# One-core adapter, diffusion, film and attention kernel: first FFN, query, key and value products as three float32r products each

## What is computed

```python
scale, shift = split(silu(sin_emb(timestep)) @ W_ada + b_ada)
x = ln(src) * (1 + scale) + shift
q, k, v = x @ Wq + bq, x @ Wk + bk, x @ Wv + bv          # 16 heads of 16
probs = softmax(where(src_mask, -inf, q @ k.T / 4 + attention_bias))
x = x + (probs @ v) @ Wo + bo
h = ln(x) * g2 + beta2
out = x + gelu2(h @ W1 + b1) @ W2 + b2                   # 256 -> 1024 -> 256
```

## Time and profile before

| what | us |
| --- | --- |
| median of 3 runs | 933.13 (932.63 to 935.77) |
| span of the profiled execution, first to last instruction | 929.6 |
| before the first head's exponentials | 93.2 |
| turn 0 | 96.0 |
| turns 1 to 6, each | 104.4 to 104.6 |
| last turn and what follows it | 113.5 |
| PE, DVE, ACT, POOL busy | 856.0, 742.4, 727.5, 237.6 |

### The profile page before, as it was taken

How to read it: one execution, slowest core, us unless ns; L and a number is a source line. 1 busy time by engine, 2 the same in 40 slices (tenths; PEclk the granted TensorE clock), 3 DMA queues, 4 the chain that set the end, 5 groups by cost and what they waited for, 6 DMA issues and landing times.

```text
span 929.6 us, 18071 instructions
## 1 busy us (share of the span) xinstructions
PE 856.0 (92%) x5630; PEld 659.5 (71%) x5715; DVE 742.4 (80%) x2377; ACT 727.5 (78%) x1897; POOL 237.6 (26%) x236
## 2 busy tenths in 40 slices
PE   7775878999999999999999999999999999999987
PEld 6454656777777777777777777777777777777766
DVE  8556888898898898898898898898897898866542
ACT  1122978979898888979898888979898888988763
POOL 2232123224123323223123323223123323120000
PEclk9777899999999999999999999999999999999999
DMA  9813644554447363654447363554447363555400
GB/s 258 250 50 101 188 136 138 154 162 138 132 131 187 98 168 105 168 160 136 133 131 188 98 170 104 169 161 132 136 131 188 98 170 102 158 161 167 140 12 23
DMA packets 133081, 130.88 MB, mean 141 GB/s; under 512 B 18265, under 2 KB 123481, under 8 KB 132969
## 3 DMA queue, kind: packets, MB, share of 16 engines
q1 hardware_dynamic: 101616, 112.02, 42.9%
q10 hardware_dynamic: 31370, 17.71, 6.9%
HBM read 112.61 MB, written 17.07 MB: 140 GB/s over the span
## 4 chain that ended last, share of the span: by engine, by line
PE 58%; ACT 19%; DVE 7%; issue 3%; POOL 0%; ACTq 0%; DVEq 0%
PE ff_ps L1340 11%; PE ff_ps L1321 8%; PE PT_ps L1376 8%; ACT Pr L1073 5%; PE G L1144 5%; PE G L1136 5%; PE scores_ps L1361 4%; PE ctx_ps L1398 3%; ACT L1073 3%; DVE bias L931 2%; PE scores_ps L1358 2%; PE ff_ps L1307 2%; ACT tanh L1055 2%; ACT ffT L1059 2%; ACT PT L1086 2%
## 5 line engine op out<-in xcount | busy, mean ns | idle before, releaser
L1073 ACT ACTIVATE Pr<-bias,nmax 128x256 f32<-128x256 f32 x512 | 255.7, 506 | 35.0 <-DVE nmax L931 34.5
L931 DVE CUSTOM_DVE_ANT_0 bias<-scores_ps,bias 128x256 f32<-128x256 f32 x512 | 194.0, 420 | 48.1 <-PE scores_ps L1361 27.9
L1086 ACT ACTIVATE PT<-PT_ps 128x512 f32<-128x512 f32 x256 | 152.2, 595 | 51.8 <-PE PT_ps L1376 47.1
L1376 PE MATMUL PT_ps<-ident,Pr 128*128 128x128 f32 x1024 | 155.6, 274 | 8.0 <-ACT Pr L1073 8.0
L560 POOL TENSOR_TENSOR rstd<-var,half_neg 128x2 f32<-128x2 f32 (+1 forms) x64 | 43.2, 674 | 387.6 <-DVE var L684 252.4
L1376 PEld LDWEIGHTS PT_ps<-ident,Pr 128*128 128x128 f32 x1024 | 119.6, 140 | 16.8 <-ACT Pr L1073 13.2
L1321 PE MATMUL ff_ps<-ctxT,w 128*128 128x256 f32 x480 | 117.2, 387 | 12.8 <-ACT ffT L1059 10.7
L1340 PE MATMUL ff_ps<-w,ffT 128*128 128x256 f32 x480 | 113.1, 381 | 0.2 <-DVE ffT L908 0.2
L1321 PEld LDWEIGHTS ff_ps<-ctxT,w 128*128 128x128 f32 x480 | 86.3, 190 | 32.5 <-ACT ffT L1059 16.2
L1361 PE MATMUL scores_ps<-k_stack,q_stack 96*128 96x256 bf16 x512 | 98.7, 273 | 7.3 <-issue 2.1
L1073 ACT ACTIVATION_READ_ACCUMULATOR Pr<-bias,nmax 128x1 f32 x512 | 100.5, 196 | 0.0
(11 more groups left out here) (216 smaller groups left out, 1637.2 us busy)
## 6 DMA issues: line engine op xcount, KB each, us to landing
bias<-in_fside_Bx16xSxS_dram SPq DMA_DIRECT2D x256, 256.0 KB, 3.2
part_dram<-front ACTq DMA_DIRECT2D x32, 384.0 KB, 2.8
q_stack<-part_dram SPq DMA_DIRECT2D x32, 192.0 KB, 3.2
k_stack<-part_dram SPq DMA_DIRECT2D x32, 192.0 KB, 3.9
F<-in_x_dram SPq DMA_DIRECT2D x16, 256.0 KB, 3.7
ada<-rows_dram SPq DMA_DIRECT2D x16, 256.0 KB, 5.3
q_stack<-part_dram SPq DMA_DIRECT2D x32, 128.0 KB, 3.2
k_stack<-part_dram SPq DMA_DIRECT2D x32, 128.0 KB, 3.8
```

Of the source, the lines that this page charges most:

```text
L931: nc.vector.tensor_tensor_reduce(out=t, in0=SP_[:, n % 2, q * S:(q + 1) * S], in1=t, scale=-1.0, scalar=BIG, op0=ALU.add, op1=ALU.min, acc ...
L1073: ins = nc.scalar.activation(Pr[:, n % PR, q, :], bias[:, n // CH % RING, 2 * (n % CH) + q, :], ACT.Exp, bias=nmax[:, n, q:q + 1], scale=-1.0,
L1086: nc.scalar.activation(PT[:, m % BATCH, :, :].rearrange("p c q -> p (c q)"), TP[:, m % 2, :], ACT.Identity).then_inc(pt_ok, 1)
L1376: ins = pe.transpose(TP[:, m % 2, c * S + q * P:c * S + (q + 1) * P], Pr[:, m % PR, q, c * P:(c + 1) * P], ident[:, :])
```

## The change

- q, k, v and `w1` products: both operands are cut into a high part (rounded by a write as float32r) and the rest, also float32r, and each product is made of three float32r products, high x high, high x rest and rest x high. Moving operands stay 256 columns wide.
- The weights' parts are made once on POOL: `s_parts` for Wq, Wk, Wv and `s_w1_0` to `s_w1_3` for W1. The activations' high parts are written by ACT in place of `x4T` and `hT`, and the rests by DVE in new steps `x4T_low` and `hT_low`.
- ACT no longer adds shift and beta2. Their products with the weights are computed once on PE (`s_seq`, `s_row`) and added to the biases of q, k and the first FFN (`qkv_b`, `b1`) and to the row added to the output projection (`rows`). V is written by a copy without bv.
- `x4T` and `ctxT` hold one sequence, not two, so a write waits for the last reader of the other sequence. The stacks hold two groups of 8 heads, and every group of six DMAs waits for the scores of the group before in the same place.
- Wq, Wk, Wv and W1 are loaded into `Pr`, `PT` and `ffT`; W1 waits for `h2_mm`. `s_bq` goes.
- The tables have new slots throughout. The `WARM` table stays.

The diff, cut:

```diff
+F32R = mybir.dt.float32r
...
-AT_FIRST = {... "s_h1": (5.5, 5.5), ... "s_rows": (15.25, 15.25), ... "w_in": (16, 28.75), ... "s_bq": (7.75, 7.75)
+AT_FIRST = {... "s_h1": (2, 2), ... "s_rows": (17.25, 17.25), ... "w_in": (15.25, 27.75), ...
+            "s_seq": (12.5, 12.5), "s_row": (16, 16), "s_parts": (14, 14),
+            "s_w1_0": (34.75, 34.75), "s_w1_1": (39, 39), "s_w1_2": (40.75, 40.75), "s_w1_3": (45.25, 45.25)
-SP_AT = {"front": (0, 7), "stacks": (1, 2, 9, 11), "mask": 6, "rows": (12, 3)}
+SP_AT = {"front": (1, 3), "stacks": (1, 5, 8, 10), "mask": 12, "rows": (14, 2)}
...
-        qs = sb("q_stack", [P, H * 2 * S], BF16)
+        qs = sb("q_stack", [P, H * S], BF16)
...
+                if b or later(j):
+                    wait_alone(sp, score_mm, (2 * j + b - 1) * H + (g + 1) * GROUP)
...
+            sp.wait_ge(h2_mm, 1)
+            sp.dma_start(w1_raw, mat("L3_cond_W1")).then_inc(w1_loaded, 16)
...
+                if once("s_parts", j, n):
+                    pool.wait_ge(qkv_loaded, 8 * 16)
+                    for w in range(3):
+                        nc.gpsimd.tensor_copy(qkv_high[w][:, :, :], w_raw[w]).then_inc(qkv_parts, 1)
+                        pool.wait_ge(qkv_parts, 2 * w + 1)
+                        nc.gpsimd.tensor_tensor(qkv_low[w][:, :, :], w_raw[w], qkv_high[w][:, :, :], ALU.subtract
+                                                ).then_inc(qkv_parts, 1)
...
+                if once("s_seq", j, n):
+                    dve.wait_ge(seq_mm, 2)
...
+                for b in seqs("x4T_low", j, n):
+                    dve.wait_ge(x4T_ok, LEAD + 2 * j + b + 1)
+                    for c in range(2):
+                        ins = nc.vector.scalar_tensor_tensor(
+                            out=x4T_low[:, c, :], in0=GF[b][:, c, :], scalar=cond[:, 2 * j + b, C_ONESC + c:C_ONESC + c + 1],
+                            in1=x4T_high[:, c, :], op0=ALU.mult, op1=ALU.subtract)
...
+            def in_parts(dst, stat, moving):
+                for c in range(2):
+                    for s, x in ((0, 0), (0, 1), (1, 0)):
+                        ins = pe.matmul(dst, stat[s][:, c, :], moving[x][:, c, :],
+                                        start=(c == 0 and s == x), stop=(c == 1 and s == 1))
...
+                if once("s_seq", j, n):
+                    pe.wait_ge(cond_ok, NC)
+                    pe.wait_ge(qkv_loaded, 8 * 16)
+                    pe.wait_ge(sel_ok, 2)
+                    for w in (2, 0, 1):
+                        for m in range(2):
+                            for c in range(2):
+                                ins = pe.matmul(seq_b[:, w, m, :], w_raw[w][:, c, m * P:(m + 1) * P], cond[:, :, C_SHIFT3 + c],
+                                                start=(c == 0), stop=(c == 1))
+                    ins.then_inc(seq_mm, 1)
+                    pe.wait_ge(w1_loaded, 4 * 16)
+                    for f in range(FB):
+                        for c in range(2):
+                            ins = pe.matmul(TP[:, 0, 6 * B + f:6 * B + f + 1], w1_raw[:, c, f * P:(f + 1) * P],
+                                            beta2[:, c:c + 1], start=(c == 0), stop=(c == 1))
+                    ins.then_inc(seq_mm, 1)
...
-                    by_feature(wq, x4T[:, :, b * S:(b + 1) * S], b).then_inc(qkv_mm[0], 1)
+                    by_feature_parts(0, b).then_inc(qkv_mm[0], 1)
...
-                        for c in range(2):
-                            ins = pe.matmul(bank("w1", j, b, m)[:, e, :], w1[:, c, f * P:(f + 1) * P], ctxT[:, c, b * S:(b + 1) * S],
-                                            start=(c == 0), stop=(c == 1))
+                        ins = in_parts(bank("w1", j, b, m)[:, e, :],
+                                       [t[:, :, f * P:(f + 1) * P] for t in (w1_high, w1_low)], hT_parts)
```

More of the change, by code:

```diff
@@ new lines @@
+AT_FIRST = {"s_sin": (0.5, 0.5), "s_se": (5, 5), "s_trig": (4.25, 4.25), "s_onehot": (3.25, 3.25),
+            "s_grid": (1.25, 1.25), "s_h1": (2, 2), "s_h2": (6.5, 6.5), "s_h2t": (6.75, 6.75), "s_sel": (2, 2),
+            "s_cond": (9.25, 9.25), "s_condt": (10.5, 10.5), "s_mask": (25, 25), "s_rows": (17.25, 17.25),
+            "x4": (28.25, 44.75), "s_fill": (10, 10), "s_seq": (12.5, 12.5), "s_row": (16, 16), "s_parts": (14, 14),
+            "s_w1_0": (34.75, 34.75), "s_w1_1": (39, 39), "s_w1_2": (40.75, 40.75), "s_w1_3": (45.25, 45.25),
+            "s_w2": (31.5, 31.5), "prods_p": (0.25, 1.25), "prods": (5.5, 6), "diffs": (5.5, 12.5),
+            "edges": (5.5, 13.25), "l0": (3.25, 19.5), "x1": (5.75, 18.25), "relu": (3, 11.5), "x1_turn": (3.5, 21),
+            "x1T": (3.75, 13), "res1": (6.75, 21.75), "down": (6.25, 21.5), "hid": (5.75, 17), "expert": (6.5, 22),
[7 rows of a table added]
+            "q_out": (28, 40.75), "k": (22.5, 40.75), "kf": (28, 40.5), "k_split": (22.25, 41), "k_out": (29, 42),
+            "v": (25.5, 43), "V": (25.75, 43.5)}
@@ L220, in adapter_to_attention_kernel @@
         ew = sb("ew", [P, B, A])
-        qs = sb("q_stack", [P, H * 2 * S], BF16)
-        ks = sb("k_stack", [P, H * 2 * S], BF16)
-        stacks = [t[0:STACK, :].rearrange("p (b h n) -> p b h n", b=2, h=H) for t in (qs, ks)]
+        qs = sb("q_stack", [P, H * S], BF16)
+        ks = sb("k_stack", [P, H * S], BF16)
+        stacks = [t[0:STACK, :].rearrange("p (g h n) -> p g h n", g=2, h=GROUP) for t in (qs, ks)]
         ffT = sb("ffT", [P, FB, S])
-        x4T = sb("x4T", [P, 2, 2 * S])
+        x4T_high, x4T_low = (sb(f"x4T_{part}", [P, 2, S], F32R) for part in ("high", "low"))
+        hT_high, hT_low = (sb(f"hT_{part}", [P, 2, S], F32R) for part in ("high", "low"))
         V = sb("V", [P, 4, H // 2, PAIR_W])
@@ L904, in back @@
                     row_norm(ff_at(j, b)[:, 0:2, :], x5[:, half, :], back_mv[:, half, :], back_rstd[:, half, 0]).then_inc(hn_ok, 1)
+                for b in seqs("hT_low", j, n):
+                    dve.wait_ge(hT_ok, 2 * j + b + 1)
+                    for c in range(2):
+                        ins = nc.vector.scalar_tensor_tensor(
+                            out=hT_low[:, c, :], in0=bank("hn", j, b)[:, c, :], scalar=g2[:, c:c + 1],
+                            in1=hT_high[:, c, :], op0=ALU.mult, op1=ALU.subtract)
+                    ins.then_inc(hT_low_ok, 1)
                 for b, m in pieces("ff", j, n):
@@ L1026, in front @@
                     act.wait_ge(x3_tr, 2 * j + b + 1)
+                    if b or later(j):
+                        act.wait_ge(qkv_mm[2], 2 * j + b)
                     for c in range(2):
-                        evac(x4T[:, c, b * S:(b + 1) * S], GF[b][:, c, :], x4T_ok if c else None,
-                             scale=cond[:, 2 * j + b, C_ONESC + c:C_ONESC + c + 1], b=cond[:, 2 * j + b, C_SHIFT3 + c:C_SHIFT3 + c + 1])
+                        evac(x4T_high[:, c, :], GF[b][:, c, :], x4T_ok if c else None,
+                             scale=cond[:, 2 * j + b, C_ONESC + c:C_ONESC + c + 1])
                 for w in range(2):
                     for b in seqs(("qf", "kf")[w], j, n):
+                        if not later(j):
+                            act.wait_ge(seq_ok, 6)
                         act.wait_ge(qkv_mm[w], 2 * j + b + 1)
@@ L1046, in back @@
                     for c in range(2):
-                        evac(ctxT[:, c, b * S:(b + 1) * S], bank("hn", j, b)[:, c, :], hT_ok if c else None, scale=g2[:, c:c + 1],
-                             b=beta2[:, c:c + 1])
+                        evac(hT_high[:, c, :], bank("hn", j, b)[:, c, :], hT_ok if c else None, scale=g2[:, c:c + 1])
                 for b, m in pieces("h1", j, n):
@@ L1138, in by_feature, with by_feature_parts, by_token_parts @@
                 return ins
+            def in_parts(dst, stat, moving):
+                for c in range(2):
+                    for s, x in ((0, 0), (0, 1), (1, 0)):
+                        ins = pe.matmul(dst, stat[s][:, c, :], moving[x][:, c, :],
+                                        start=(c == 0 and s == x), stop=(c == 1 and s == 1))
+                return ins
+            x4T_parts, hT_parts = (x4T_high, x4T_low), (hT_high, hT_low)
+            def by_feature_parts(w, b):
+                for m in range(2):
+                    mine = slice(m * P, (m + 1) * P)
+                    ins = in_parts(GF[b][:, m, :], [t[w][:, :, mine] for t in (qkv_high, qkv_low)], x4T_parts)
+                return ins
+            def by_token_parts(w, b):
+                for t in range(2):
+                    mine = slice(t * P, (t + 1) * P)
+                    ins = in_parts(GF[b][:, t, :], [x[:, :, mine] for x in x4T_parts], [part[w] for part in (qkv_high, qkv_low)])
+                return ins
             def by_token(w, xT, b):
@@ L1197, in front @@
                     ins.then_inc(cond_tr, 1)
+                if once("s_seq", j, n):
[3 more added lines that the diff above has]
+                    for w in (2, 0, 1):
+                        for m in range(2):
```

(20 more changed lines are left out.)

122 lines of the change are left out of this document (67 added, 55 removed), and 50 rows, old and new, of tables (AT, AT_FIRST, AT_LAST).

## The result

| | before | after |
| --- | --- | --- |
| median, us | 932.88 (931.90 to 935.77) | 957.16 (956.29 to 958.89) |
| span of the profiled execution | 929.6 | 956.9 |
| before the first exponentials | 93.2 | 107.8 |
| turn 0 | 96.0 | 100.1 |
| turns 1 to 6, each | 104.4 to 104.6 | 105.7, one of 106.7 |

The ratio after to before is 1.0251 [1.0231, 1.0270]: slower by 24.3 us, where 21 us faster was forecast. The stages are those of one profiled execution each. Their spans differ by 27.3 us, 3 more than the medians, because the profiled execution of the kernel before was a short one and that of the changed kernel the longest of its four (958.89).

What follows compares the result with a forecast made beforehand. PE was taken to bound the kernel, busy 101.0 of 104.6 us a turn. Span 929.6 + 8 (start) - 1 (turn 0) - 24 (turns 1 to 6) - 4 (end) = 908.6; with 3.5 to the median, 912 us, range 898 to 931.

Steps and rivals of the forecast that it cites:

- The 3.5 us between span and median: Whole kernel: the median was taken to lie 3.5 us above the profiled span, so 908.6 became 912.
- The turn after: Turns 1 to 6: each falls from 104.5 to 100.5 us, -4.0 x 6 = -24; bounds per turn -5.4 and -1.0.
- PE's products: q, k, v and `w1`: 84 float32r products at 0.112 us a sequence, 2.7 us less PE a sequence, 5.4 a turn.
- DVE's new work: `x4T_low` and `hT_low`: eight operations a turn at 0.44 us each, +3.5 us; DVE goes to 94.2 busy, 97.4 with gaps.
- other products fill PE meanwhile: Full turns: a rest step adds some 0.9 us to its sequence's chain before q and `w1`, while PE has other products.
- The ring: Stacks of two groups of heads: costed at nothing; if its cover went, a turn would pay a slot, 3.3 us.
- POOL's cutting of Wq, Wk and Wv: In the start: three weights cut in 5.7 us, ending near 54, needed by q near 80, so hidden.
- The start: Before the first exponentials: `s_seq`'s 56 weight-load records delay `w_in` by 8.5 us (bounds +5.0 and +12.5); in all +8.
- Turn 0: First turn: 3.9 us less PE work against DVE's rests and POOL's cutting of W1; taken as -1 (-3.9 to +5).
- The end: The last 113.5 us: less PE work in `w1`, q, k and v, one bare rest step; -4 (-5 to -2).
- Rival B: Full turns: DVE becomes the bound at 94.2 busy, a turn comes to 103, 928 us in all; chance 0.18.

Runs made afterwards that it cites:

- three cuts together: Kernel before with half of `w1`'s contraction, the third part of q and k, and half of the eviction of q and k left out: 909.75 us.
- less PE: Kernel before with half of the contraction of `w1`, the first FFN product, left out from pair 1 on: 926.77 us.

## Why the prediction was wrong

Against the span of 908.6 in the forecast's sum, 48.3 us are missing: turns 1 to 6 give 32.3, the start 6.6, turn 0 5.1, and the end 4.3. The 3.5 us between span and median was not what lies around the first and last instruction: in a timed run of the kernel before that is 2.0 (933.31 against a span of 931.3), and the rest was the luck of a short profiled execution.

- **The turn after is the step that failed.** The forecast took PE's busy share of 96.5% as proof that PE bounds a turn, and so as a rate at which the next engine could also be filled (97.4/0.965). A cut of 5.2 us on PE in the kernel before moves its turn by 0.9 at most, and in the changed kernel cuts of 4.2 and 6.5 us don't shorten it, though at a lower clock. What the runs show in its place is a turn in which the in-order queues of PE, DVE and ACT hold each other up: three cuts together give 2.9 where their sum is 0.8 to 1.4, and behind head 23 a wait of PE for DVE is passed through ACT to the next head. That wait alone was followed through the queues. For the other heads the tie is argued from the sums. The -4.0 a turn was (635.2 - 626.9)/6 = +1.4, from the sums of turns 1 to 6.
- **PE's products** were right in kind and mis-sized. In a turn of before they are 15.6 + 7.7 + 3.8 = 27.1 us busy and after 23.1, so -3.9, not -5.4: 0.117 a record instead of 0.112, and a longer first record behind each wait.
- **DVE's new work** was counted well (0.475 to 0.480 each), and its busy time rose by just 0.3, mainly since the operations L968, L699 and L921 (0.74, 0.48 and 0.42) take less than before (0.91, 0.65 and 0.58). The error was to price it by DVE's total. What counts is where in DVE's queue it stands, and which heads stand behind it there or behind the product that waits for it: 1.9 us a turn in the new slots, 6.0 in the old. That "other products fill PE meanwhile" was wrong too: PE waits 3.5 us a turn for these steps, and behind head 23 the next head pays 0.9 of it.
- **The ring** cost nothing, as said, and neither did POOL's cutting of Wq, Wk and Wv, which ended at 53.5 us, long before q.
- **The start** was the dear end of its own bounds. The 56 records took 12.0 us (taken 9.2), the warm ones 3.5 (taken 2.4), because the clock didn't rise; q's rest step then cost 2.9 of waiting where 1.0 was taken. The +8 was +14.6 between these two executions and some +10.5 between the middles of all with either start, so about 4 of the 6.6 are chance.
- **Turn 0** has +4.1, within its bounds (-3.9 to +5). Without the rest steps of pair 1 it took 97.5. What of the remainder is POOL's cutting of W1 and what is a low clock (0.91 against 0.95) wasn't separated.
- **The end** gave nothing instead of -4. PE has 3.2 us less in the last turn and the turn is no shorter; with the rest steps out it was 81.3 + 29.9 instead of 82.9 + 30.8.

Rival B was the nearest in kind, and its price was still too low: it let the turn fall to 103. No case had a turn that grows without an engine being full.

No kernel tried here beats the one before with the whole computation in it. The changed kernel would have to win back 24 us, and even without any rest step from pair 1 on it takes 938.9.

## What to carry to other kernels

A high busy share on one engine (96.5% here) doesn't make it the bound where in-order queues hand each other short pieces: cut some work on that engine alone and look at the length of a turn, then cut all together, before building a faster version of its work. Price a new step on a shared queue by what stands behind it in that place, not by the engine's idle total; here the price was 1.9 us a turn in slots made for it and 6.0 in others. Set-up work that is all weight loads should be priced at the low clock: the 56 records ran at it in every trace that has them in the start. Moving 32 of them out of the start into turn 0 saved nothing in all (957.14 against 957.16).

## What was not expected of the hardware

- A PE that was busy without a break from 52 to 62 us with one-column products and then warm ones stayed at 1.2 GHz; in the kernel before the clock's mean was 0.98 from 48.7 to 50.0 us. With the old slots, and without rest steps, PE was busy for all of 45 to 60 us with the same products, and the mean clock was 0.50 there too; over 52 to 62 it was 0.58 and 0.60, so it rose shortly before 62.
- Less work on PE brought a lower clock in places where it had been at 2.4 GHz. In the longer turn of less PE, the clock goes down in the second of these rows and stays down in the third; PE was busy for 3.6 and 3.0 of 5 us in the first two:

```profile
429.00:434.00 5.00, 3.61 (x32) 2.27 (x32) 4.76 (x16) 4.99 (x15) 0.70 (x1) 1.00 0.57 154
434.00:439.00 5.00, 3.00 (x16) 1.97 (x15) 4.45 (x17) 3.68 (x11) 1.50 (x2) 0.88 0.63 179
439.00:444.00 5.00, 5.00 (x29) 4.22 (x29) 3.94 (x14) 4.96 (x12) 2.80 (x3) 0.78 0.68 191
```

  That turn, with this dip in it, is 1.3 us longer than its neighbour, so part of what is saved on PE is given back.
- A DVE operation of 128x256 with its operands in SBUF took 478 ns in one place and 1103 in another (a mean of four), where POOL worked on operands in SBUF at the same time. The same operation with one operand in PSUM took 475 there. The Trainium skill (GPSIMD Engine Reference, Specifications) states that POOL's SBUF interface is shared with VectorE and contended by instructions with two SBUF inputs; these two numbers agree with it.
